# Blank rows written in 64 pieces on the sync engine's queue, and a routing phase re-ordered with one-pass products

## The chip, the core and the metric

One core of one Trainium2 chip runs the whole program. The metric is the device time of one execution in microseconds (us). The engines are TensorE (PE for products, PEld for its weight loads), VectorE (DVE), ScalarE (ACT), GpSimd (POOL) and the sync engine (SP), which here only issues DMAs. SP and POOL each have a DMA queue of their own; 16 DMA engines serve both.

## The reference

Two decoder layers over 64 sequences ("blocks") of 128 tokens and 256 features, all in float32:

```
x = x + mamba(layernorm(x))                  # layer 0: state-space mixer, 8 heads
x = x + cross_attention(layernorm(x), ctx)   #          16 heads with rotary positions
x = x + recurrence(layernorm(x))             #          gated recurrence over the 64 blocks
x = x + attention(layernorm(x))              # layer 1: grouped attention
x = x + cross_attention(layernorm(x), ctx)   #          one head of 256
x = x + experts(layernorm(x))                #          8 experts, 2 per token, one shared
```

The last line is the one that the routing phase serves:

```
scores = sigmoid(xf @ gate_w.T + lb_bias);  topw, topi = top_k(scores, 2)
topw = topw / (topw.sum(-1, keepdims=True) + 1e-8)
for e in range(8):
    m = topi == e
    wmean = (topw * m).sum() / max(m.sum(), 1)
    out = out + where(m.any(-1), mlp_e(xf) * wmean, 0)
out = out + mlp_shared(xf)
```

## The kernel before

The program is five phases, each with its own streams of instructions for the engines and a barrier of all engines at its end.

**start** loads and turns weights. **layer0** is a software pipeline over the 64 blocks (`pipeline` with `step(i)`: stage k of the pipeline works on block i - k), with a fixed hand-written order on every engine. **layer1** is a second such pipeline. **route** handles all 8192 tokens at once. **experts** first computes the shared expert for each block and scatters every token's row to the place in `pair_rows` (a DRAM buffer of 512 features and 4 further words per row) where tokens with the same pair of experts stand together; then it runs over 91 slots of 128 such rows and scatters the results to the output.

A slot may be filled only in part, so `pair_rows` must first hold blank rows: zeros, and a token number past the last one, so that the output's scatter drops them. In layer0 POOL does this: it fills the tiles `blank` and `blank_end` (L1460 to L1463), and issues 12 DMAs (L1469), 4 strided quarters of the buffer with three column ranges each, for 92 x 128 rows in all. Only behind these does POOL's stream come to its first step of the pipeline, `scale_tokens(0)` (L1477, L1480), which multiplies the mixer's inputs `m_xt_` of a block by their step sizes. TensorE's `m_mix` (L943) needs that product.

SP's step in layer0 has three parts: `load_sums(i)` (L881, 512 KB, a row of decay sums sent to all partitions of `m_E`; it waits for the mixer's products and squares of block i - 1), `store_output(i - 4)` (L890, which waits for ScalarE's last stage), and `load_context(i)` (L886, 128 KB). VectorE uses the sums at the start of its next step (`m_relative`, L1294), ahead of `m_residual` (L1330), the statistics, and the convolution (`m_convolve`, L1268, which waits for ScalarE's taps, L1108).

In route VectorE runs one chain in which nearly every instruction waits for the one before it (`link`). It waits for the constant table (L2127), builds the scores, the two best experts of each token and the number of its pair of experts (28 pairs), and from that `t_hot`, 64 x 28 ones and zeros per partition (L2143). TensorE counts each pair's tokens in each block (28 products of one column, L2078), VectorE spreads the counts with a triangular mask (L2147), and TensorE makes every token's rank among its pair (L2083, L2084: four groups of two float32 products of 448 columns each) and the pairs' totals (L2086). One semaphore, `t_rank`, releases VectorE behind all nine. VectorE then computes each pair's first slot (L2150 to L2156), the place of each token (L2159 to L2166), the slots' owners (L2167 to L2170), the shares and their sums per expert (L2172 to L2178), and, after a product that adds these over partitions (L2089), the mean weights (L2180 to L2187) and the owners' row (L2190).

Of the kernel before, what the change touches and what calls it, by code (L numbers as in the profile page):

```python
# [55 lines left out]
BLANKS = 4 * -(-SLOTS // 4)  # L56
# [4 lines left out]
def constant_table():  # L61
# [59 lines left out]
        t_table t_chain t_sig t_hot t_tiles t_prefix t_rank t_sums t_tot t_owner t_ownT  # L121
# [10 lines left out]
def decoder(nc, args, xo_dram, cum_dram, table, out):  # L132
# [8 lines left out]
    with ExitStack() as stack:  # L141
# [608 lines left out]
        slots = nc.dram_tensor("pair_rows", (BLANKS * P, ROW), F32, kind="Internal").ap()  # L750
# [122 lines left out]
        with phase("layer0") as block:  # L873
            @block.sync
            def _(e):
# [15 lines left out]

                def step(i):
# [566 lines left out]
            def _(e):  # L1459
# [56 lines left out]
                e.wait_ge(S["blank"], 12 * 16)  # L1516
# [526 lines left out]
        def by_pair(a):  # L2043
            return a.rearrange("p (b q) -> p b q", q=PAIRS)

        t_hot, t_prod = (by_pair(wk(NB * PAIRS)) for _ in range(2))
# [22 lines left out]
        with phase("route") as block:  # L2069
# [5 lines left out]
            def _(e):  # L2075
                e.wait_ge(S["t_hot"], 1)
                for q in range(PAIRS):
                    last = e.matmul(bank[7][0:NB, SPARE + q:SPARE + q + 1], t_hot[:, :, q], const[:, C_ONE:C_ONE + 1],  # L2078
                                    start=True, stop=True)
                last.then_inc(S["t_tiles"], 1)  # L2080
                e.wait_ge(S["t_prefix"], 1)
                for g in range(4):
                    e.matmul(bank[4 + g][:, 0:SPARE], r_up, t_hot[:, 16 * g:16 * g + 16, :], start=True, stop=False)  # L2083
                    e.matmul(bank[4 + g][:, 0:SPARE], const[0:NB, C_ONE:C_ONE + P], t_prod[0:NB, 16 * g:16 * g + 16, :],  # L2084
                             start=False, stop=True)
                e.matmul(bank[4][:, SPARE:SPARE + PAIRS], const[0:NB, C_ONE:C_ONE + P], t_tiles[0:NB], start=True, stop=True)\  # L2086
# [471 lines left out]
```

## Time and profile before

| | us |
|---|---|
| median of 3 runs | 3533.28 |
| lowest, highest | 3522.47, 3534.46 |
| the profiled execution | 3528.69 |
| its span | 3526.9 |

The span is the time that the profile's clock covers, 1.8 us less than the execution's own time. Of it TensorE is busy 88%, VectorE 79%, ScalarE 64%, POOL 43%. The phase layer0 begins near 91 us, route near 3022 us, and experts near 3087 us. A timeline row gives start, duration, engine, line, operation, and in brackets how long the engine had been idle before it and what released it; rows that follow each other on an engine with the same line are merged, with their number behind the x. PEclk is TensorE's granted clock as a share of 2.4 GHz.

### The profile page before, as it was taken

The page shows a single profiled execution, that of the slowest core. Times are in us where ns is not written, and L with a number is a line of the kernel's source. Part 1 is how long each engine was busy: PE and PEld are TensorE (multiplying, and loading weights), DVE is VectorE, ACT ScalarE, POOL GpSimd, SP SyncE. Part 2 cuts the span into 40 slices and gives each one's busy share as a digit, 9 for nine tenths or more (in the row PEclk, how much of TensorE's full clock was granted, in tenths as well). Part 3 has the DMA queues.
Part 4 walks back from the last instruction along what each step waited for, and adds up shares of the span by engine and source line. Part 5 has one row for each costly group of instructions (what it writes and reads, how often), then busy time and mean ns, then how long its engine had stood idle before and what let it go on. Part 6 is the DMA issues. An engine that isn't in the chain of part 4 may idle for free. (4 is left out here: it accounts for less than half of the span.)

```text
span 3526.9 us, 95395 instructions
## 1 busy us (share of the span) xinstructions
PE 3097.6 (88%) x27092; PEld 2670.7 (76%) x27093; DVE 2780.0 (79%) x8725; ACT 2267.1 (64%) x8246; POOL 1532.2 (43%) x5125
## 2 busy tenths in 40 slices
PE   6149999999999999999998689999999999399998
PEld 4047888888888888888887577777777777287998
DVE  5148888888888888888886478888888887488776
ACT  4026777777777777777776477777777777033333
POOL 1124445444444444544443145555555554033333
PEclk9569999999999999999999799999999999599999
DMA  6930000100100000000010100000000000022443
GB/s 181 218 84 28 32 27 28 34 27 27 36 27 27 33 30 27 30 33 27 27 36 14 59 18 16 18 18 15 18 18 18 15 18 14 2 88 109 136 139 91
DMA packets 92223, 162.13 MB, mean 46 GB/s; under 512 B 13379, under 2 KB 57776, under 8 KB 92144
## 3 DMA queue, kind: packets, MB, share of 16 engines
q1 hardware_dynamic: 73616, 102.32, 9.8%
q0 software_dynamic: 18528, 58.84, 5.7%
q8 instruction: 39, 0.64, 0.1%
q14 instruction: 40, 0.33, 0.0%
HBM read 102.85 MB, written 61.79 MB: 47 GB/s over the span
## 5 line engine op out<-in xcount | busy, mean ns | idle before, releaser
L386 POOL TENSOR_TENSOR tiny<-tiny 128x1 f32<-128x1 f32 x3456 | 779.6, 226 | 801.1 <-DVE tiny L373 560.4
L803 ACT ACTIVATE work<-bank,att 128x128 f32<-128x128 f32 x2048 | 722.2, 378 | 57.2 <-DVE att L793 51.2
L803 ACT ACTIVATION_READ_ACCUMULATOR work<-bank,att 128x1 f32 x2048 | 445.3, 217 | 0.0
L793 DVE TENSOR_REDUCE att<-bank 128x4 f32<-128x512 f32 x512 | 334.2, 684 | 45.6 <-PE bank L786 45.6
L822 PE MATMUL bank<-const,work 128*128 128x128 f32 x2048 | 317.1, 278 | 22.3 <-ACT work L803 18.2
L786 PEld LDWEIGHTS bank<-work 32*128 32x128 f32 x4096 | 253.7, 189 | 107.0 <-issue 74.6
L1268 DVE SCALAR_TENSOR_TENSOR work<-work,small 128x127 f32<-128x127 f32 (+2 forms) x1152 | 318.7, 345 | 9.9 <-ACT work L1108 5.2
L786 PE MATMUL bank<-work 32*128 32x128 f32 x4096 | 302.4, 286 | 20.1 <-ACT work L1153 2.5
L386 POOL TENSOR_TENSOR tiny<-tiny,const 128x1 f32<-128x1 f32 x1152 | 248.2, 215 | 90.2
L822 PEld LDWEIGHTS bank<-const,work 128*128 128x128 f32 x2048 | 238.6, 142 | 61.9 <-ACT work L803 38.7
L186 PE MATMUL bank<-w1r,workr 128*128 (+2 forms) x802 | 267.8, 334 | 0.4 <-issue 0.2
L186 PE MATMUL bank<-w0r,workr 128*128 128x256 f32 (+1 forms) x640 | 215.1, 336 | 43.9 <-DVE workr L1248 40.5
L206 PE MATMUL bank<-extra,w0p 128*128 128x128 f32 x1536 | 244.1, 282 | 2.8 <-ACT r_tfi_ L1169 1.8
L188 PE MATMUL bank<-w1r,workr 128*128 (+2 forms) x802 | 241.8, 302 | 0.0
L187 PE MATMUL bank<-w1r,workr 128*128 (+2 forms) x802 | 241.7, 301 | 0.0
L206 PE MATMUL bank<-d_state,w0p 128*128 128x128 f32 x1536 | 236.9, 277 | 0.0
L943 PE MATMUL bank<-work 128*128 128x64 f32 x1024 | 135.1, 278 | 90.0 <-POOL work L1477 88.7
L206 PEld LDWEIGHTS bank<-extra,w0p 128*128 128x128 f32 x1536 | 205.0, 194 | 11.3 <-ACT r_tfi_ L1169 2.1
L206 PEld LDWEIGHTS bank<-d_state,w0p 128*128 128x128 f32 x1536 | 205.0, 194 | 0.0
L943 PEld LDWEIGHTS bank<-work 128*128 128x128 f32 x1024 | 130.9, 201 | 90.9 <-issue 89.0
L188 PE MATMUL bank<-w0r,workr 128*128 128x256 f32 (+1 forms) x640 | 196.5, 307 | 0.0
L187 PE MATMUL bank<-w0r,workr 128*128 128x256 f32 (+1 forms) x640 | 196.2, 307 | 0.0
(357 smaller groups left out, 8486.2 us busy)
## 6 DMA issues: line engine op xcount, KB each, us to landing
work<-decay_sums SPq DMA_DIRECT2D x64, 512.0 KB, 3.6
pair_rows<-extra POOLq DMA_DIRECT2D x8, 2944.0 KB, 27.8
work<-pair_rows SPq DMA_DIRECT2D x91, 258.0 KB, 2.8
work<-in_ctx SPq DMA_DIRECT2D x128, 128.0 KB, 2.0
x_res<-in_x POOLq DMA_DIRECT2D x8, 1024.0 KB, 17.5
recurrence_out<-r_xo_ SPq DMA_DIRECT2D x64, 128.0 KB, 1.7
work<-recurrence_out SPq DMA_DIRECT2D x64, 128.0 KB
out_dram<-work POOLq DMA_INDIRECT x91
```

The lines of the kernel that those rows point to most:

```text
L186: pe.matmul(out_, lhs[0], rhs[0], start=first, stop=False)
L187: pe.matmul(out_, lhs[0], rhs[1], start=False, stop=False)
L188: return pe.matmul(out_, lhs[1], rhs[0], start=False, stop=last)
L206: last = pe.matmul(out_, w[:, k, n0:n0 + P], act[:, k, :], start=first and k == 0, stop=last_ and k == 1)
L386: e.tensor_tensor(out_, a_, b_, ALU.add if b_ is three_halves else ALU.mult)\
L786: mm = e.matmul(sc_banks[g % 2][:, c:c + P], qT[32 * g:32 * g + 32, odd, blk, :], kT[32 * g:32 * g + 32, blk, :], start=True, stop=True)
L793: e.tensor_reduce(a_nm[:, 4 * g:4 * g + 4], sc_banks[g % 2][:, :].rearrange("p (h k) -> p h k", k=P), AX.X, ALU.max, negate=True).then_inc ...
L803: last = e.activation(Pb[g % 2][:, c * P:c * P + P], sc_banks[g % 2][:, c * P:c * P + P], ACT.Exp, bias=a_nm[:, 4 * g + c:4 * g + c + 1], ...
L822: last = e.transpose(pt_banks[g % len(pt_banks)][:, h * P:h * P + P], Pb[g % 2][:, h * P:h * P + P], ident)
L943: last = e.matmul(bank[0][:, h * HD:h * HD + HD], m_E[:, h, :], m_xdt_[:, h * HD:h * HD + HD], start=True, stop=True)
L1268: last = e.scalar_tensor_tensor(out=m_acc[:, j, k:P], in0=m_raw_[:, j, 0:P - k], scalar=cw[:, j, CONV - 1 - k:CONV - k], in1=m_acc[:, j, k:P],
```

## The change

The buffer has 91 slots in place of 92, since each piece covers 91 x 128 / 64 = 182 rows. POOL still fills `blank` and `blank_end`, but its 12 DMAs, and its wait for them at the end of the phase, are gone. SP waits for the two tiles ahead of its pipeline, writes one piece of 182 rows in every step behind `load_context(i)`, with three DMAs, and waits for all 192 at the end.

```
-                e.wait_ge(S["blank_ready"], 2)
-                for k in range(4):
-                    rows_k = slots.rearrange("(s k p) d -> k p s d", k=4, p=P)[k]
-                    for at, n, of in ((0, D, blank), (D, D, blank), (2 * D, 4, blank_end)):
-                        e.dma_start(rows_k[:, :, at:at + n], of.unsqueeze(1).to_broadcast([P, BLANKS // 4, n]))\
-                            .then_inc(S["blank"], 16)
+                def blank_rows(b):
+
+                    n = SLOTS * P // NB
+                    rows_b = slots[0:NB * n].rearrange("(b p s) d -> b p s d", b=NB, p=n // 2)
+                    rows_b = rows_b[b] if isinstance(b, int) else rows_b[ds(b, 1)].rearrange("o p s d -> p (o s) d")
+                    for at, n_, of in ((0, D, blank), (D, D, blank), (2 * D, 4, blank_end)):
+                        e.dma_start(rows_b[:, :, at:at + n_], of[0:n // 2].unsqueeze(1).to_broadcast([n // 2, 2, n_]))\
+                            .then_inc(S["blank"], 16)
+
                     if live(b):
                         load_context(b)
-
+                    b = i
+                    if live(b):
+                        blank_rows(b)
+
+                e.wait_ge(S["blank_ready"], 2)
                 pipeline(e, 4, step)
                 e.wait_ge(S["r_store"], 16 * NB)
+                e.wait_ge(S["blank"], 3 * 16 * NB)
```

In route, `t_hot`, the counts and the masked counts are written as float32r in `w_s` and `workr` (the values are small whole numbers), with float32r copies of the ones and of the triangle that ScalarE makes. The ranks' groups go to banks 0 to 3, each with a count of `t_rank` of its own.

```
             def _(e):
+                e.wait_ge(S["t_ones"], 1)
                 e.wait_ge(S["t_hot"], 1)
                 for q in range(PAIRS):
-                    last = e.matmul(bank[7][0:NB, SPARE + q:SPARE + q + 1], t_hot[:, :, q], const[:, C_ONE:C_ONE + 1],
+                    last = e.matmul(bank[7][0:NB, SPARE + 2 * q:SPARE + 2 * q + 2], r_hot[:, :, q], r_one[:, 0:2],
                                     start=True, stop=True)
                 last.then_inc(S["t_tiles"], 1)
                 e.wait_ge(S["t_prefix"], 1)
+                e.matmul(bank[4][:, SPARE:SPARE + PAIRS], r_one[0:NB], r_tiles[0:NB], start=True, stop=True)\
+                    .then_inc(S["t_whole"], 1)
                 for g in range(4):
-                    e.matmul(bank[4 + g][:, 0:SPARE], r_up, t_hot[:, 16 * g:16 * g + 16, :], start=True, stop=False)
...
+                    e.matmul(bank[g][:, 0:SPARE], r_below, r_hot[:, 16 * g:16 * g + 16, :], start=True, stop=False)
+                    e.matmul(bank[g][:, 0:SPARE], r_one[0:NB], r_before[0:NB, 16 * g:16 * g + 16, :],
+                             start=False, stop=True).then_inc(S["t_rank"], 1)
...
             def _(e):
                 e.activation(t_s, logits, ACT.Exp, scale=-1.0).then_inc(S["t_sig"], 1)
+                e.activation(r_one, const[:, C_ONE:C_ONE + P], ACT.Copy)
+                e.wait_ge(S["t_table"], 16)
+                e.activation(r_below, r_up, ACT.Copy).then_inc(S["t_ones"], 1)
```

VectorE's wait for the table stands just ahead of `t_hot`; the shares stand behind it, the owners, the shares' sums and the two comparisons with the experts' numbers behind the pairs' first slots, and the last products and sums of the mean weights have no `link` between the two halves.

What stands in a row on SP in the loop of layer0 before:

```order
L881 ISA
L881 DMA work<-decay_sums 128x1024
L889 REGISTER_ALU
L890 ISA
L890 DMA recurrence_out<-r_xo_ 128x256
L886 ISA
L886 DMA work<-in_ctx 128x256
L179 REGISTER_ALU
```

and now:

```order
L880 ISA
L880 DMA work<-decay_sums 128x1024
L888 REGISTER_ALU
L889 ISA
L889 DMA recurrence_out<-r_xo_ 128x256
L885 ISA
L885 DMA work<-in_ctx 128x256
L897 ISA
L897 DMA pair_rows<-extra 182x1x256
L897 ISA
L897 DMA pair_rows<-extra 182x1x256
L897 ISA
L897 DMA pair_rows<-work 182x1x4
L178 REGISTER_ALU
```

Three DMAs stand between a block's context and the next block's decay sums, which the loop comes to next.

On POOL, at the start of layer0, before (the last rows are `scale_tokens(0)`):

```order
L1463 IOTA work 128x1
L1469 DMA pair_rows<-extra 128x23x256
L1469 DMA pair_rows<-extra 128x23x256
L1469 DMA pair_rows<-work 128x23x4
L1469 DMA pair_rows<-extra 128x23x256 x2
L1469 DMA pair_rows<-work 128x23x4
L1469 DMA pair_rows<-extra 128x23x256 x2
L1469 DMA pair_rows<-work 128x23x4
L1469 DMA pair_rows<-extra 128x23x256 x2
L1469 DMA pair_rows<-work 128x23x4
L1477 TENSOR_TENSOR work<-work,tiny 128x512
```

and now:

```order
L1476 IOTA work 128x1
L1484 TENSOR_TENSOR work<-work,tiny 128x512
L1487 TENSOR_TENSOR work<-work,small 128x512
```

Nothing of POOL's own stands ahead of the first block's work any more.

On VectorE, in route, from the counts to the places of the tokens, now:

```order
L2169 TENSOR_TENSOR workr<-work,w_s 64x1792
L2174 TENSOR_SCALAR work<-bank 128x28
L2175 TENSOR_SCALAR work<-work 128x28
L2176 TENSOR_SCALAR work<-work 128x28
L2178 TENSOR_TENSOR work<-work 128x28 x5
L2180 TENSOR_TENSOR work<-work 128x28
L2181 TENSOR_TENSOR work<-work 128x28
L2183 TENSOR_TENSOR work<-work 128x27 x2
L2184 TENSOR_REDUCE work<-work 128x2
L2186 TENSOR_REDUCE work<-work 128x8
L2187 TENSOR_REDUCE work<-rows 128x8
L2189 TENSOR_TENSOR work<-const,work 128x512 x2
```

L2181 to L2189 stood behind the places before; now they stand ahead of the first instruction that needs the ranks.

## Rows read from the trace of the kernel before

**Rows 1.** Stretches: length; busy PE, PEld, DVE, ACT, POOL (instructions); PEclk; DMA share; GB/s.
```profile
108.00:199.00 91.00, 1.54 (x6) 1.25 (x6) 3.23 (x5) 2.02 (x4) 10.78 (x8) 0.50 0.89 195
...
3022.00:3086.00 64.00, 22.20 (x78) 11.75 (x78) 36.15 (x68) 0.63 (x1) 0.00 (x0) 0.50 0.01 2
```

**Rows 2.** Waits by engine, line and releaser, 92 to 320 us: total, times, longest.
```profile
PE bank L943 <- POOL work L1477: 88.7, 1, 88.7
...
DVE work L1294 <- DMA work<-decay_sums: 11.8, 2, 9.0
```

**Rows 3.** Timeline of POOL, start of layer0.
```profile
146.99 1.48 POOL L1469 DMA_DIRECT2D pair_rows<-work  x1 [47.35 <-issue]
...
195.59 1.48 POOL L1469 DMA_DIRECT2D pair_rows<-extra  x1 [41.21 <-issue]
...
198.57 1.05 POOL L1477 TENSOR_TENSOR work<-work,tiny 128x512 f32<-128x512 f32 x1
```

**Rows 4.** Timeline of all engines, blocks 0 and 1 of layer0.
```profile
110.61 0.60 ACT L1125 ACTIVATE work<-bank 128x512 f32<-128x512 f32 x1 [2.20 <-PE bank L932]
...
205.67 0.33 SPq L881 DMA_DIRECT2D work<-decay_sums  x1
...
214.69 2.41 ACT L1108 ACTIVATE work<-work,small 128x128 f32<-128x128 f32 x6
216.41 0.87 DVE L1294 TENSOR_SCALAR work<-work,tiny 128x128 f32<-128x128 f32 x4 [9.04 <-DMA work<-decay_sums]
...
219.62 5.02 DVE L1268 SCALAR_TENSOR_TENSOR work<-work,small 128x127 f32<-128x127 f32 x18
```

**Rows 5.** Timeline of one steady step of layer0.
```profile
1016.63 0.33 SPq L886 DMA_DIRECT2D work<-in_ctx  x1
...
1018.94 0.33 SPq L881 DMA_DIRECT2D work<-decay_sums  x1
...
1023.70 0.88 DVE L1294 TENSOR_SCALAR work<-work,tiny 128x128 f32<-128x128 f32 x4
...
1025.67 0.48 DVE L1330 SCALAR_TENSOR_TENSOR x_res<-bank,tiny,x_res 128x256 f32 x1 [0.76 <-POOL tiny L386]
...
1045.64 0.33 SPq L881 DMA_DIRECT2D work<-decay_sums  x1
```

**Rows 6.** Line L881, the decay sums' load (64 issues).
```profile
DMA to landing us min/median/max: 3.3/3.6/10.7
```

**Rows 7.** Timeline of route: ScalarE and VectorE up to the counts.
```profile
3022.19 0.63 ACT L2098 ACTIVATE work<-tab 128x512 f32<-128x512 f32 x1 [2.76 <-PEq L157]
...
3026.43 0.42 DVE L2131 TENSOR_SCALAR work<-work 128x512 f32<-128x512 f32 x1
...
3042.41 6.55 PEld L2078 LDWEIGHTS bank<-const,work 128*64 128x64 f32 x56 [22.01 <-DVE work L2143]
```

**Rows 8.** Timeline of VectorE in route, from the counts on.
```profile
3049.08 0.18 DVE L2146 TENSOR_SCALAR work<-bank 64x28 f32<-64x28 f32 x1 [6.73 <-PE bank L2078]
...
3066.06 0.19 DVE L2150 TENSOR_SCALAR work<-bank 128x28 int32<-128x28 f32 x1 [14.74 <-PE bank L2086]
...
3068.06 2.21 DVE L2159 SCALAR_TENSOR_TENSOR work<-work,bank 128x448 f32<-128x448 f32 x4
...
3074.53 0.18 DVE L2167 TENSOR_TENSOR work<-work 128x28 f32<-128x28 f32 x1
...
3075.32 0.22 DVE L2172 TENSOR_TENSOR work<-work 128x64 f32<-128x64 f32 x1
...
3077.84 1.07 DVE L2177 TENSOR_REDUCE work<-work 128x8 f32<-128x512 f32 x1
...
3080.70 0.17 DVE L2180 TENSOR_SCALAR work<-bank 128x8 f32<-128x8 f32 x1 [0.70 <-PE bank L2089]
```

**Rows 9.** Timeline of TensorE, float32r products of 512 columns right after route.
```profile
3090.77 0.63 PE L188 MATMUL bank<-w1r,workr 128*128 128x512 f32 x1
3091.20 0.63 PE L186 MATMUL bank<-w1r,workr 128*128 128x512 f32 x1
```

More of the change, by code:

```diff
@@ L748, in decoder @@
         r_T = wk(D).rearrange("p (k t) -> p k t", k=2)
-        slots = nc.dram_tensor("pair_rows", (BLANKS * P, ROW), F32, kind="Internal").ap()
+        slots = nc.dram_tensor("pair_rows", (SLOTS * P, ROW), F32, kind="Internal").ap()
         blank, blank_end = wk(D), wk(4)
@@ L1515, in _ @@
                 pipeline(e, 5, step)
-                e.wait_ge(S["blank"], 12 * 16)
         layer0_weights.close()
@@ L2044, in by_pair @@
             return a.rearrange("p (b q) -> p b q", q=PAIRS)
-        t_hot, t_prod = (by_pair(wk(NB * PAIRS)) for _ in range(2))
+        t_prod = by_pair(wk(NB * PAIRS))
+        r_hot = by_pair(w_s[:, 0:NB * PAIRS])
+        t_hot = r_hot.bitcast(F32)
+        at_ = NB * PAIRS
+        r_one, r_below, r_tiles = w_s[:, at_:at_ + P], w_s[:, at_ + P:at_ + 2 * P], w_s[:, at_ + 2 * P:at_ + 2 * P + PAIRS]
+        r_before = by_pair(wr(NB * PAIRS))
         t_s, t_first, t_second = (by_tile(wk(NT)) for _ in range(3))
@@ L2126, in _ @@
                     e.memset(ends, 0.0)
-                e.wait_ge(S["t_table"], 16)
-                e.tensor_scalar(where[:, :, 2].bitcast(I32), r_tok, 1.0, None, ALU.mult)
                 e.wait_ge(S["t_sig"], 1)
@@ L2166, in _ @@
                 e.tensor_scalar(where[:, :, 3].bitcast(I32), t_place, 1.0, None, ALU.mult)
-                link(e.tensor_tensor(t_gone, r_slot.to_broadcast([P, PAIRS]), t_ends[5][:, HALF:], ALU.is_ge))
-                for c in range(2):
-                    link(e.tensor_tensor(t_step[:, c, 0:PAIRS - 1], t_gone[:, 0:PAIRS - 1], r_step[c], ALU.mult))
-                e.tensor_reduce(t_owner, t_step[:, :, 0:PAIRS - 1], AX.X, ALU.add).then_inc(S["t_owner"], 1)
-                link(e.tensor_tensor(t_rcp, t_max, t_max2, ALU.add))
-                link(e.tensor_scalar(t_rcp, t_rcp, 1e-8, None, ALU.add))
-                link(e.reciprocal(t_rcp, t_rcp))
-                link(e.tensor_tensor(t_s, t_s, t_mask, ALU.mult))
-                link(e.tensor_tensor(t_s, t_s, wide(t_rcp), ALU.mult))
-                link(e.tensor_reduce(t_sums[:, 0:E], t_s.rearrange("p b e -> p e b"), AX.X, ALU.add))
-                e.tensor_reduce(t_sums[:, E:2 * E], t_mask.rearrange("p b e -> p e b"), AX.X, ALU.add).then_inc(S["t_sums"], 1)
                 e.wait_ge(S["t_tot"], 1)
@@ L2183, in _ @@
                                             in1=t_mean[:, E:2 * E], op0=ALU.mult, op1=ALU.mult))
-                for c, key in enumerate((t_upper, t_lower)):
-                    link(e.tensor_tensor(t_tmp, across(const[:, C_IOTA:C_IOTA + E]), wide(key), ALU.is_equal))
-                    link(e.tensor_tensor(t_tmp, t_tmp, across(t_mean[:, 0:E]), ALU.mult))
-                    link(e.tensor_reduce(where[:, :, c], t_tmp, AX.X, ALU.add))
+                for c, is_ in enumerate((t_first, t_second)):
+                    e.tensor_tensor(is_, is_, across(t_mean[:, 0:E]), ALU.mult).then_inc(S["t_chain"], 1)
+                for c, is_ in enumerate((t_first, t_second)):
+                    n += 1
+                    e.wait_ge(S["t_chain"], n)
+                    e.tensor_reduce(where[:, :, c], is_, AX.X, ALU.add)
                 e.wait_ge(S["t_ownT"], 1)
```

43 lines of the change are left out of this document (28 added, 15 removed).

## The prediction

> **What bounds the kernel now.** I read the profile in three steps. First the busy time by stretch. TensorE is busy 88% of the span, so most of the program is a full pipeline; what matters are stretches in which every engine is idle. Two stand out [rows 1]: from 108 to 199 us nothing computes (TensorE 1.5 us busy of 91, VectorE 3.2) while the DMA engines are 89% busy, and from 3022 to 3086 us, the routing phase, VectorE is busy 36 of 64 us and TensorE 22, at a granted clock of 0.50, the lower of its two levels (1.2 GHz). The change touches just these two, and adds work to a third stretch, the steady steps of layer0, which are 1045.64 - 1018.94 = 26.7 us each [rows 5].
>
> Second, who ends the first hole. The list of waits says that TensorE's mixer product L943 waited 88.7 us, once, for POOL's L1477 [rows 2]. POOL's own timeline shows why: its blank-row DMAs take 1.48 us each to issue, but twice its stream stands still in the middle of them, 47.35 and 41.21 us, with no other engine named [rows 3]: I read this as waiting for room in its queue. Only at 198.57 us does it come to L1477, although L1477's input, ScalarE's L1125, was there at 110.61 + 0.60 = 111.21 us [rows 4].
>
> Third, the waits inside route: VectorE stands 6.73 us for the counts and 14.74 us for ranks and totals [rows 8].
>
> **The change, part 1: the first block.** POOL has only two memsets and an iota ahead of L1477, so this starts when its input is there, at about 111.3 us instead of 198.57: **-87.3 us**. What follows at once (L943) waited for L1477 alone, so all of it moves. What is late next is block 1's decay sums. They were issued at 205.67 and VectorE waited 9.04 us for them, to 216.41 [rows 4], since they took 10.7 us to land against a median of 3.6 [rows 6]: the last blank DMAs were still running. With 3.6 us they land 7.1 us sooner, but the convolution (219.62) also needs ScalarE's taps, which end at 214.69 + 2.41 = 217.10 whatever the sums do. So the step gains at most 219.62 - 217.10 = **-2.5 us**. The new wait of SP for the blank tiles comes before its first load and delays it by under 1 us; what depends on that load ends in L1268 of block 0, which waits for the taps anyway. I cost it at nothing, at most +0.7.
>
> **Part 2: 61 steady steps.** The blanks have not gone; SP writes them, three DMAs per step. The nearest issue costs are 0.33 us each [rows 5], and setting each address adds up to 0.1 as the rows of SP's own loop stand (ISA ahead of DMA), so 1.3 us in all, behind the context's DMA, whose issue ends at 1016.96. The next decay sums were issued at 1018.94, a gap of 1.98. The issue cost therefore fits with 0.7 us to spare; SP's next instruction, and all queued behind it, is as early as now.
>
> The data also share the DMA engines with these sums. A piece is 182 rows x 2064 bytes = 376 KB. The same rows went out before at 195 GB/s with 89% of the engines' time, that is 219 GB/s at full use [rows 1], so a piece takes 1.7 us. The sums are 524 KB: 2.4 us at that rate, of their 3.6 us, so about 1.2 us passes before data flow. The piece then flows from 1018.2 to 1019.9, and the sums from 1020.1: they hardly meet. If the whole piece stood ahead, the sums would land 1.7 us late. What covers this: they land at 1018.94 + 3.6 = 1022.5, VectorE comes to them at 1023.70 (L1294) with no wait, 1.2 us later, and then idles 0.76 us for POOL at L1330 [rows 5]. So **1.9 us** of lateness costs VectorE nothing that it doesn't wait for now. If the cover goes, each microsecond more costs up to 61 us over the phase. I take +2.5 us in total for the odd collision; bounds 0 and, at 0.5 us per step beyond the cover, +30.
>
> The DMA's rows are 91 partitions read twice and 182 rows written. The Trainium skill (DMA: Bandwidth & Descriptors, section "Why a DMA increments its semaphore by 16 and not by 1") says that a DMA of the sync queue runs on the largest number up to 16 of DMA engines that divides the outermost size of both sides, which here is 13. By it the piece takes 16/13 as long, 2.1 us instead of 1.7 as an estimate from the same row, and the time of the forecast stays. No row of this trace shows it, since the DMAs of layer0 have 128 rows.
>
> **Part 3: route.** Durations by VectorE's timeline, step by step.
> - Table: L2131 starts at 3026.43, behind the table's DMA and a copy; the scores' input, ScalarE's L2098, ends at 3022.82 [rows 7]. It can start near 3022.9: **-3.5 us**. The table is now needed some 15 us later and has long landed. ScalarE's two copies end well before too.
> - Counts: 56 weight loads in 6.55 us, two for each float32 product, 0.117 each [rows 7]. A float32r product has one load and one pass, so 28 x 0.117 = 3.3, plus 0.2 for the semaphores: 3.5 instead of 6.73, **-3.2 us**. Below this the shares set the end: L2172 to L2176, 3075.32 to 3077.84 = 2.5 us [rows 8], plus a copy, now run in this wait, so they leave the chain: **-2.5 us**.
> - Ranks: VectorE waited 14.74 us for L2086, the ninth product. Now the pairs' totals come first, one product of 28 columns: I take 0.6 us. **-14.1 us**. Behind it TensorE has eight products of 448 columns. Float32r products of 512 columns follow each other in 0.43 us at this clock [rows 9], so 448 columns take 0.38 and eight 3.0, 5 us at most if each weight load adds to it. VectorE has until then: first slots 3066.06 to 3068.06 (2.0), owners 3074.53 to 3075.32 (0.8), sums 3077.84 to 3080.0 (2.1) [rows 8], and two comparisons of about 0.65: 6.2 us. So the ranks are there first, and owners and sums cost what they did.
> - The end: the wait of 0.70 us for the sums' product [rows 8] is covered by the tokens' places, **-0.7**, and four links less save **-0.4**.
>
> Route together: 3.5 + 3.2 + 2.5 + 14.1 + 0.7 + 0.4 = **24.4 us** of 64.
>
> **Sum.** 3528.7 (the profiled execution) - 87.3 - 2.5 - 24.4 + 2.5 = **3417 us**. The median of the runs before is 4.6 us above that execution and their lowest 6.2 below, so the same holds for the outcome within about 5 us.
>
> **Rivals.**
> - *Cover partly gone.* The sums land later than 1.9 us in each step: 0.5 us beyond it costs 61 x 0.5 = 30, 3447 us. For it: the pieces go out directly ahead of them, and a step had none there before. Against it: the gap of 1.98 us on SP, and 1.2 us before VectorE looks [rows 5]. 12%.
> - *Slower than before.* The same place, but the piece holds the queue for long: the 1 KB writes of SP's queue run at a quarter of the rate seen on POOL's, 6.8 us a piece, from 1018.2 to 1025.0. The sums start 4.9 us late, less the cover of 1.9 is 3.0, times 61 is 183: 3528.7 - 114.2 + 183 = 3598 us. It turns the sign where the sums land 3.8 us late (1.9 beyond the cover, 61 x 1.9 = 116), a piece of 5.7 us. Against it: the rate at which the same rows left before [rows 1], 1.7 us a piece. 3%.
> - *The hole is only moved.* Something else holds block 0, an input that the wait for POOL hid, so that 55 of the 87 us come back: 3450. Against it: L943's wait names POOL alone, and L1477's own input was 87 us early [rows 2, 4]. 3%.
> - *Route falls short.* The float32r products of few columns run no faster than the float32 ones did. Counts and half of the ranks' time return, 10 us: 3427. 5%.
> - Forecast as it stands: 77%.
>
> **How the numbers follow.** The range must reach from the full gain with no collision and the clock held up by a shorter idle time (3400) to the first rival with some more (3458). It leaves the slower rival out, and the rare case between. A measurement of this kernel tells about 0.5% from no change, 18 us. Faster by more than that: all cases but the slower one and a little of the first beyond its price, 0.96; within it 0.01; slower 0.03.
>
> **What would show it.** L1477 of block 0 near 112 us, and no stretch of idle engines after it; block 1's L1294 waits about 2 us or less. In a steady step SP's load of the sums still issues about 2 us behind the context's, lands within 5.5 us, and VectorE does not wait for it; the step stays as long as it is. Route takes 40 us, with a wait of some 3.5 us at the counts, under 1 us at the totals and none at the ranks. I am wrong if VectorE's L1294 waits for the decay sums in every step, or if POOL is late for another reason.

## The result: 3413.5 us for 3533.0, and where the time went

| | before | after |
|---|---|---|
| median | 3533.02 | 3413.51 |
| lowest, highest | 3522.47, 3534.46 | 3412.63, 3418.98 |
| the profiled execution | 3528.69 | 3413.31 |
| its span | 3526.9 | 3411.5 |

The ratio of the mean times is 0.967, with an interval of 0.965 to 0.969 (the ratios below are of means too, and the times are medians). The forecast was 3417 in a range of 3400 to 3458. Between the two profiled executions the span fell by 115.4 us. The starts of the phases (first DMA of layer0, first instructions of layer1, route and experts) divide it:

| part | before | after | difference | forecast |
|---|---|---|---|---|
| start phase | 91.26 | 93.04 | +1.8 | 0 to +0.7 |
| layer0, first step (blocks 0 and 1) | 137.35 | 47.70 | -89.65 | -89.8 |
| layer0, steps 2 to 4 | 93.44 | 87.48 | -6.0 | 0 |
| layer0, 59 steps | 26.698 each | 26.779 each | +5.1 | +2.5 |
| layer0, last steps | | | -1.5 | 0 |
| layer1 | 1046.6 | 1046.1 | -0.6 | 0 |
| route | 64.61 | 39.52 | -25.1 | -24.4 |
| experts | 440.0 | 440.6 | +0.5 | 0 |

The steps are measured between the issues of two context loads on SP. The length given for a steady step, here and below, is the mean of the last 58 of the 59; the difference in the table is that of all 59. Three readings of the profile after carry this table.

**The hole is gone.** Timeline of all engines of the changed kernel, blocks 0 and 1 of layer0 (start, duration, engine, line, what it does, and in brackets how long the engine was idle before it and for whom):

```profile
112.18 1.04 POOL L1484 TENSOR_TENSOR work<-work,tiny 128x512 f32<-128x512 f32 x1 [19.17 <-ACT work L1138]
...
119.80 0.34 SPq L880 DMA_DIRECT2D work<-decay_sums  x1
...
123.17 0.87 DVE L1307 TENSOR_SCALAR work<-work,tiny 128x128 f32<-128x128 f32 x4 [1.69 <-DMA work<-decay_sums]
...
131.75 0.35 DVE L1281 SCALAR_TENSOR_TENSOR work<-work,small 128x127 f32<-128x127 f32 x1 [4.73 <-ACT work L1121]
```

POOL's first work of block 0, which stood at 198.57 [rows 3], now waits for ScalarE and starts with its input, at 112.18. Block 1's decay sums are waited for 1.69 us, where it was 9.04 [rows 4], and the convolution behind them waits for ScalarE's taps (L1121), as the forecast said. The windows show it by engine. Stretches of the changed kernel: length; busy PE, PEld, DVE, ACT, POOL (instructions); PEclk; DMA share; GB/s:

```profile
108.00:130.00 22.00, 15.22 (x68) 13.10 (x68) 11.45 (x31) 5.61 (x12) 6.82 (x25) 0.57 0.07 25
...
141.00:169.00 28.00, 21.11 (x126) 17.51 (x126) 19.97 (x56) 14.25 (x47) 9.34 (x28) 0.76 0.13 37
169.00:197.00 28.00, 21.55 (x183) 17.44 (x183) 21.61 (x63) 18.69 (x63) 10.04 (x29) 0.94 0.13 38
197.00:228.60 31.60, 28.66 (x255) 24.89 (x254) 27.27 (x84) 24.37 (x83) 17.08 (x51) 1.00 0.10 34
...
2927.00:2967.00 40.00, 11.65 (x47) 7.64 (x47) 32.95 (x65) 1.52 (x4) 0.00 (x0) 0.50 0.02 4
```

In 22 us from 108 on TensorE is busy 15.2, where it was 1.5 in 91 [rows 1]. The middle three rows are steps 2 to 4; the same three of the kernel before:

```profile
228.00:256.00 28.00, 20.74 (x128) 16.33 (x127) 20.22 (x57) 14.25 (x48) 9.48 (x28) 0.80 0.07 25
256.00:287.00 31.00, 24.61 (x182) 19.93 (x181) 21.38 (x63) 18.59 (x63) 10.31 (x29) 0.83 0.06 22
287.00:322.00 35.00, 32.18 (x260) 28.31 (x258) 27.65 (x85) 25.09 (x84) 17.09 (x52) 0.90 0.06 20
```

The work is the same, but the granted clock reaches 0.94 and 1.00 in the second and third of them where it was 0.83 and 0.90. That is where the -6.0 us lie; two other executions of the same layer0, `changed_again` and `pieces_alone`, don't have them (below).

**The steady steps have a new wait, which hardly costs anything.** Timeline of SP and VectorE of the changed kernel, one steady step:

```profile
1005.07 0.34 SPq L885 DMA_DIRECT2D work<-in_ctx  x1
1005.59 2.01 SPq L897 DMA_DIRECT2D pair_rows<-extra  x2
1007.81 0.89 SPq L897 DMA_DIRECT2D pair_rows<-work  x1
1009.29 0.35 SPq L880 DMA_DIRECT2D work<-decay_sums  x1
...
1012.74 0.87 DVE L1307 TENSOR_SCALAR work<-work,tiny 128x128 f32<-128x128 f32 x4 [0.73 <-DMA work<-decay_sums]
```

and waits of VectorE (232 to 1860 us) and of TensorE (229 to 1809 us) in the same kernel, as total, times, longest:

```profile
DVE work L1307 <- DMA work<-decay_sums: 56.3, 59, 1.3
...
DVE x_res L1343 <- POOL tiny L385: 1.7, 2, 1.4
```

```profile
PE bank L821 <- ACT work L802: 7.6, 28, 0.5
```

Before, VectorE's waits of the same stretch (320 to 1960 us) had no decay sums among them, but

```profile
DVE x_res L1330 <- POOL tiny L386: 46.3, 60, 1.4
```

The sums were issued 1018.94 - 1016.63 = 2.31 us behind the context [rows 5] and are now issued 4.22 behind it, 1.91 later. They land in the usual time from their issue (line L880, issue to landing):

```profile
DMA to landing us min/median/max: 3.3/3.6/4.2
```

So VectorE waits some 0.95 us for them in each step, and in exchange no longer waits 0.77 us for POOL a moment later. What is left reaches TensorE in some of the steps as a short wait for ScalarE (L802), and these steps are the longer ones: the 28 steps with such a wait take 26.90 us on average, the 31 without it 26.68.

**Route.** VectorE's first instruction in route, before:

```profile
3022.25 0.36 DVE L2126 MEMSET work<- 128x44 f32 x6 [1.55 <-PEq L157]
```

Timeline of VectorE and TensorE of the changed kernel, from the first instruction to the places of the tokens:

```profile
2931.40 0.36 DVE L2141 MEMSET work<- 128x44 f32 x6 [1.54 <-PEq L156]
2932.00 0.43 DVE L2143 TENSOR_SCALAR work<-work 128x512 f32<-128x512 f32 x1 [0.24 <-ACT work L2110]
...
2948.05 3.32 PEld L2090 LDWEIGHTS bank<-w_s 128*64 128x64 f32 x28 [18.49 <-issue]
...
2951.56 0.18 DVE L2167 TENSOR_SCALAR w_s<-bank 64x28 fp32r<-64x28 f32 x1 [1.12 <-PE bank L2090]
...
2954.28 0.19 DVE L2174 TENSOR_SCALAR work<-bank 128x28 int32<-128x28 f32 x1 [0.48 <-PE bank L2094]
...
2954.84 0.28 PEld L2098 LDWEIGHTS bank<-workr,w_s 64*128 64x128 f32 x1 [0.38 <-issue]
2954.84 0.74 PE L2098 MATMUL bank<-workr,w_s 64*128 64x448 f32 x1
...
2958.86 0.74 PE L2098 MATMUL bank<-workr,w_s 64*128 64x448 f32 x1
...
2960.25 2.20 DVE L2193 SCALAR_TENSOR_TENSOR work<-work,bank 128x448 f32<-128x448 f32 x4
```

The wait for the counts fell from 6.73 to 1.12 us, that for ranks and totals from 14.74 to 0.48 [rows 8], and the instruction that needs the ranks (2960.25) waits for nothing. In the window 2927 to 2967 above, VectorE is busy 33 of 40 us; it was 36 of 64 [rows 1].

### The profile page after: what moved, and what is told of

Same layout as the page of the kernel before. It is cut to its first block and busy times, and to the rows that moved or that the text cites. A ratio compares the mean times of both kernels' runs of the same rounds, so it can differ in the third digit from the quotient of the medians.

```text
span 3411.5 us, 95859 instructions
## 1 busy us (share of the span) xinstructions
PE 3081.2 (90%) x27055; PEld 2659.9 (78%) x27056; DVE 2776.1 (81%) x8725; ACT 2258.2 (66%) x8248; POOL 1512.2 (44%) x5113
## 5 line engine op out<-in xcount | busy, mean ns | idle before, releaser
L385 POOL TENSOR_TENSOR tiny<-tiny 128x1 f32<-128x1 f32 x3456 | 773.3, 224 | 800.0 <-DVE tiny L372 559.2
L802 ACT ACTIVATE work<-bank,att 128x128 f32<-128x128 f32 x2048 | 720.1, 377 | 55.9 <-DVE att L792 50.1
L802 ACT ACTIVATION_READ_ACCUMULATOR work<-bank,att 128x1 f32 x2048 | 444.5, 217 | 0.0
L821 PE MATMUL bank<-const,work 128*128 128x128 f32 x2048 | 317.9, 278 | 30.6 <-ACT work L802 25.8
L385 POOL TENSOR_TENSOR tiny<-tiny,const 128x1 f32<-128x1 f32 x1152 | 251.6, 218 | 90.2
L205 PE MATMUL bank<-extra,w0p 128*128 128x128 f32 x1536 | 242.9, 281 | 3.0 <-ACT r_tfi_ L1182 1.7
L205 PE MATMUL bank<-d_state,w0p 128*128 128x128 f32 x1536 | 235.7, 276 | 0.0
L205 PEld LDWEIGHTS bank<-extra,w0p 128*128 128x128 f32 x1536 | 203.7, 193 | 11.4 <-ACT r_tfi_ L1182 2.1
L205 PEld LDWEIGHTS bank<-d_state,w0p 128*128 128x128 f32 x1536 | 203.9, 193 | 0.0
L1501 POOL TENSOR_TENSOR x_res<-x_res,rows 128x256 f32 (+1 forms) x64 | 46.7, 729 | 343.4 <-DVE work L1264 343.4
L205 PE MATMUL bank<-work,w0p 128*128 128x128 f32 x1536 | 185.6, 278 | 0.5 <-ACT work L1107 0.5
```

The costliest lines, as they stand in the source:

```text
L205: last = pe.matmul(out_, w[:, k, n0:n0 + P], act[:, k, :], start=first and k == 0, stop=last_ and k == 1)
L385: e.tensor_tensor(out_, a_, b_, ALU.add if b_ is three_halves else ALU.mult)\
L802: last = e.activation(Pb[g % 2][:, c * P:c * P + P], sc_banks[g % 2][:, c * P:c * P + P], ACT.Exp, bias=a_nm[:, 4 * g + c:4 * g + c + 1], ...
L821: last = e.transpose(pt_banks[g % len(pt_banks)][:, h * P:h * P + P], Pb[g % 2][:, h * P:h * P + P], ident)
L1501: e.tensor_tensor(x_res[:, ds(b * D, D)], x_res[:, ds(b * D, D)], bo2_row, ALU.add).then_inc(S["c_x1b"], 1)
```

## The experiments

The kernels ran in three groups, each on one chip with the kernel before beside it. Group 1, `pieces_alone`, `route_alone`, `pieces_behind_sums` and `pieces_192`: before 3525.2 us (3518.0 to 3531.2). Group 2, `changed_again`, `pieces_behind_sums_again`, `one_dma_piece` and `one_dma_behind_sums`: 3538.4 (3526.8 to 3542.3). Group 3, the other four: 3526.3 (3523.3 to 3531.2).

**One half at a time.** `pieces_alone` is the kernel before with the blank rows in pieces, and the old route:

```diff
+                    b = i
+                    if live(b):
+                        blank_rows(b)
...
-                for k in range(4):
-                    rows_k = slots.rearrange("(s k p) d -> k p s d", k=4, p=P)[k]
```

> The kernel before with the blank-row part of the change alone; route as before. Theory (the parts add, layer0 gave 92 us and route 25): 3413.5 + 25 = 3438 us. Rival (part of the 25 us in route came from layer0's pieces, for instance by another granted clock or buffer): clearly off 3438 by more than 5 us. In its profile route should again last 64.6 us from the first memset to the first instruction of experts, and the steps of layer0 should jitter between 26.6 and 27.1 us as they do in the changed kernel.

Measured: 3440.8 us (3439.6 to 3443.3), ratio 0.976 [0.974, 0.978].

`route_alone` is the changed kernel with POOL's 12 DMAs back:

```diff
-                    b = i
-                    if live(b):
-                        blank_rows(b)
...
+                for k in range(4):
+                    rows_k = slots.rearrange("(s k p) d -> k p s d", k=4, p=P)[k]
```

> The changed kernel with POOL's 12 large blank DMAs put back; route as changed. Theory: 3533 - 25 = 3508 us; the hole of 88 us is back in front of L1477's successor, the steady steps are 26.70 us each without jitter, and route lasts 39.5 us. Rival (the two parts share a gain): under 3500 or over 3516.

Measured: 3506.4 us (3503.5 to 3508.0), ratio 0.994 [0.993, 0.996]. The hole was back (first step 137.03 us), and the steady steps were 26.730 us with no wait for sums. In `pieces_alone` the steps were 26.779 us as in the changed kernel, with 53.7 us of waits for sums in 59 steps. The two gains are 84.4 and 18.8 us, together 103 of about 116 (3.3% of that chip's 3525). Both times lie near the expected 3438 and 3508, but these were worked out from 3533 and 3413; against this chip's 3525 each gain is smaller than expected, 84 for 95 and 19 for 25. Of the missing 13 us 8.8 are seen in one place of the profiled executions: steps 2 to 4 of `pieces_alone` took 31.2, 30.6 and 34.5 us, 96.3 together against 87.5 in the profile after. The rest isn't settled. Route took 39.52 us in `route_alone`, as in the changed kernel, but 63.08 in `pieces_alone`, where 64.6 was expected: VectorE waited 2.19 us for the constant table there and 3.71 before, with the same instructions. So 1.5 of the 25.1 us depend on when the table lands in an execution of the old route. The two halves act in separate phases, and both are needed for the whole.

**What delays the sums: SP's issue time, or the data?** Four kernels tell them apart. `pieces_behind_sums` issues the same three DMAs behind the sums' load in the step:

```diff
                         load_sums(b)
+                        blank_rows(b)
...
-                    b = i
-                    if live(b):
-                        blank_rows(b)
```

> The changed kernel with the three DMAs of a piece moved on SP from behind the context's load to behind the decay sums' load, ahead of the wait of some 20 us for ScalarE's last stage. Theory (the pieces' issue time of 3 x 0.9 us on SP makes the next sums late, which uses up VectorE's cover and makes the steps jitter): VectorE's waits for the sums in the steady steps go from 56 us to about 0, its 46 us of waits for POOL at the residual come back, the steps are 26.70 us again, and the time falls by 58 x 0.085 = 5 us, to 3408. Rival (the jitter comes from the DMA traffic or from memory, wherever it is issued): the waits for the sums go but the steps stay at 26.79 us and the time at 3413.

Measured: 3414.1 us (3411.3 to 3414.5), ratio 0.968 [0.966, 0.970]; steps 26.729 us. The steps are nearly those of the theory (26.70); the time is not its 3408, and the changed kernel did not run on this chip to compare it with. Timeline of its SP:

```profile
1013.04 0.34 SPq L885 DMA_DIRECT2D work<-in_ctx  x1
1015.33 0.34 SPq L880 DMA_DIRECT2D work<-decay_sums  x1
1015.85 2.02 SPq L897 DMA_DIRECT2D pair_rows<-extra  x2
```

The three issues take as long as ever, but the sums are on time (2.29 us behind the context), VectorE's waits for them are 0.4 us in all and its wait for POOL is back, 46.6 us in 60 times. TensorE's new waits for L802 are gone.

`pieces_192` keeps the place and makes a piece of 192 rows (96 partitions twice) in place of 182 (91 twice):

```diff
+BLANKS = 96
...
-        slots = nc.dram_tensor("pair_rows", (SLOTS * P, ROW), F32, kind="Internal").ap()
+        slots = nc.dram_tensor("pair_rows", (BLANKS * P, ROW), F32, kind="Internal").ap()
...
-                    n = SLOTS * P // NB
+                    n = BLANKS * P // NB
```

> The changed kernel with a buffer of 96 slots, so that a piece is 96 partitions x 2 = 192 rows instead of 91 x 2 = 182; DMAs and their place as they are. Theory A (a count of rows that 16 doesn't divide is what makes an issue on SP cost 0.90 us against 0.33 of a load of 128 rows): issues near 0.35 us, VectorE's waits for the sums fall from 1 us per step to under 0.2, and the time falls by about 5 us to 3408. Theory B (the source's third dimension or the number of rows makes it): issues stay near 0.9 us or rise with 192/182 to 0.95, time 3413 to 3416.

Measured: 3413.2 us (3405.8 to 3417.1), ratio 0.967 [0.965, 0.970]; steps 26.732 us. Timeline of its SP:

```profile
1012.89 0.34 SPq L886 DMA_DIRECT2D work<-in_ctx  x1
1013.41 1.40 SPq L898 DMA_DIRECT2D pair_rows<-extra  x2
...
1016.16 0.34 SPq L881 DMA_DIRECT2D work<-decay_sums  x1
```

With 5% more rows, a DMA takes 0.6 to 0.7 us to issue in place of 0.9 to 1.05. That lies between the two theories, 0.35 and 0.9, and the time is again not the 3408 of theory A. The sums are 3.27 us behind the context, 0.96 later than before, and this is inside the 1.2 us by which they used to be early: VectorE waits 5.3 us for them, 15 times. The change of size that adds data takes the wait away, so it is the issue time that makes it.

`one_dma_piece` keeps the place and 182 rows, but writes a whole row from one tile, in one DMA:

```diff
-        blank, blank_end = wk(D), wk(4)
+        blank = layer0_weights.enter_context(nc.sbuf_tensor("blank_row", [P, ROW], F32))[:, :]
+        blank_end = blank[:, 2 * D:ROW]
...
-                    for at, n_, of in ((0, D, blank), (D, D, blank), (2 * D, 4, blank_end)):
-                        e.dma_start(rows_b[:, :, at:at + n_], of[0:n // 2].unsqueeze(1).to_broadcast([n // 2, 2, n_]))\
-                            .then_inc(S["blank"], 16)
+                    e.dma_start(rows_b, blank[0:n // 2].unsqueeze(1).to_broadcast([n // 2, 2, ROW])).then_inc(S["blank"], 16)
```

> The changed kernel with a tile of one whole blank row (516 words), so that a piece is one DMA of 182 rows of 2064 bytes instead of three; its place, behind the context's load, is as changed. Theory (what made the sums late is SP's time to issue three DMAs, 2.7 us, more than the gap of 2.0): one issue of 0.9 us fits the gap, VectorE's waits for the sums fall from 56 us to under 10, steps are 26.73 us flat, and the time is 3 to 5 us under changed_again. Rival (the piece's data ahead of the sums make them late): waits of 0.5 us or more per step remain, since the bytes are the same.

Measured: 3410.7 us (3406.8 to 3417.1), ratio 0.964 [0.963, 0.966]; steps 26.710 us. Its SP, and VectorE's waits (232 to 1860 us):

```profile
1001.82 0.34 SPq L886 DMA_DIRECT2D work<-in_ctx  x1
1002.35 0.92 SPq L897 DMA_DIRECT2D pair_rows<-blank_row  x1
1004.13 0.35 SPq L881 DMA_DIRECT2D work<-decay_sums  x1
```

```profile
DVE work L1306 <- DMA work<-decay_sums: 22.6, 57, 2.1
```

VectorE's waits fell to 22.6 us, not to the expected 10 or less: both the theory and its rival hold in part. One issue costs what each of three did, so the sums are issued on time, 2.31 us behind the context. But now they take longer to land. Line L881 of this kernel, 400 to 1800 us:

```profile
DMA to landing us min/median/max: 4.7/5.0/6.6
```

That is 1.3 to 1.4 us over the 3.6 and 3.7 of the others: this is what the piece's data do when they stand directly ahead of the sums. Both mechanisms exist; in the changed kernel the slow issues spread the data out so far that only the first acts.

`one_dma_behind_sums` joins both edits:

```diff
                         load_sums(b)
+                        blank_rows(b)
...
+                    e.dma_start(rows_b, blank[0:n // 2].unsqueeze(1).to_broadcast([n // 2, 2, ROW])).then_inc(S["blank"], 16)
```

> Both edits: one DMA per piece, and that behind the decay sums' load. Theory: nothing is left to gain beyond either alone, steps 26.73 us, 3 to 5 us under changed_again. It is the version that I would expect to be the fastest by a little.

Measured: 3412.8 us (3405.3 to 3413.9), ratio 0.964 [0.963, 0.965]; steps 26.697 us, one wait for sums of 0.4 us. It is not the fastest by anything that the times can tell.

To compare these closely, the changed kernel (`changed_again`) and `pieces_behind_sums` ran again on that same chip, unaltered.

> The changed kernel again, beside the three below on one chip. In the profile that I have of it, the three steps after the first block took 28.4, 27.3 and 31.8 us (granted clock 0.76, 0.94, 1.00), in four other kernels' profiles 31.2, 30.6 and 34.6 with the same instructions. Theory (the clock rises at another time from run to run, worth up to 9 us, and this is most of the scatter): its steady steps average 26.78 us in any case, and the time lies between 3408 and 3420. Rival (the short steps belong to this kernel): they are again under 29 us.

Measured: 3421.2 us (3413.3 to 3425.2), ratio 0.966 [0.965, 0.968]; steps 26.843 us, 59.8 us of waits for sums; steps 2 to 4 took 31.1, 30.5 and 31.8 us, 93.4 together, at granted clocks of 0.66, 0.80 and 1.00. The median is 1 us above the expected 3408 to 3420, and the steps are longer than 26.78.

> The three DMAs of a piece behind the decay sums' load, again, beside the changed kernel on the same chip. Its steady steps were 26.73 us flat, those of the changed kernel jitter around 26.79. Theory (the late sums cost VectorE 3.5 to 5 us over the phase): 3 to 5 us under changed_again. Rival (nothing that a time can show): within 2 us of it.

Measured: 3411.8 us (3405.8 to 3414.1), ratio 0.963 [0.962, 0.965]; steps 26.716 us.

Beside each other, the changed kernel is 8.3 to 10.5 us above the three versions of this group that let the sums go on time or nearly so. The 59 steps account for 7.3 to 8.4 us in the profiled executions, where 3 to 5 had been expected. The two kernels with one DMA also had short steps 2 to 4 in their profiles (87.7 and 87.5 us), so the clean pair is `changed_again` and `pieces_behind_sums_again`, both with 93.4 or 93.5: their profiled executions are 8.3 us apart, 7.3 of it in the 59 steps. The whole difference is 0.3%, and only the interval of `pieces_behind_sums_again` lies clear of the changed kernel's, by 0.0001; the steps' lengths and waits, which agree in all runs, bear it better than the medians.

**Another place for the same DMAs.** `pieces_on_pool` gives the pieces to POOL, behind its last mixer work of the step:

```diff
                         scale_tokens(b)
+                        blank_rows(b)
```

> The changed kernel with the same 64 pieces issued by POOL on its own queue, behind each block's scale_tokens, instead of by SP. It asks whether the pieces or the other queue removed the hole. Theory (POOL stood still because its queue had no room for more than five of the large DMAs; pieces of 182 rows leave room): L1477's successor starts near 112 us, no wait of POOL at an issue of more than 2 us, and 3413 to 3425, since three issues of 0.6 to 1.5 us per step now stand in front of POOL's roots, for which VectorE waits 0.76 us a step already; if 1.5 us each, up to 58 x 2 = 116 us slower than that. Rival (POOL's issuing as such holds it up, whatever the size): hole or long waits in every step, over 3500.

Measured: 3483.9 us (3476.5 to 3484.2), ratio 0.988 [0.986, 0.990]. No hole (first step 47.38 us), but steps of 27.866 us, so the time is well above the 3413 to 3425 of the theory and inside what it allowed for slow issues. Timeline of its POOL, and VectorE's longest waits over the whole span:

```profile
1011.63 1.41 POOL L1471 DMA_DIRECT2D pair_rows<-extra  x2
1012.83 0.92 POOL L1471 DMA_DIRECT2D pair_rows<-work  x1
1013.42 0.86 POOL L385 TENSOR_TENSOR tiny<-tiny 128x1 f32<-128x1 f32 x2
```

```profile
DVE work L1250 <- POOL tiny L385: 96.4, 63, 4.7
```

The 2.3 us of issues stand ahead of the inverse roots (L385) that VectorE waits for, and 1.1 to 1.2 us of them come through in each step. The same DMAs cost 2.7 us on SP (three of 0.9), of which 0.09 to 0.14 comes through. What matters is who is queued behind them, not how long they take.

`bulk_on_sp` leaves them in 12 large DMAs, issued by SP behind its work of the first step:

```diff
+                def blank_all():
+                    e.wait_ge(S["blank_ready"], 2)
+                    for k in range(4):
...
+                pipeline(e, 4, step, 0, blank_all)
```

> The changed kernel with the 12 large blank DMAs (92 x 128 rows) back, but issued by SP behind step 0 of its pipeline. It asks whether the hole came from POOL being held, or from the traffic of 24 MB in front of the next loads. Theory (both: with POOL free, L1477's successor starts near 112 us, but block 1's decay sums stand behind 24 MB in SP's queue until about 200 us): the hole moves to VectorE's wait for the sums, the time is within 15 us of 3413 + 80 = 3493. Rival (POOL's standing still was all): block 1 goes on as in the changed kernel, under 3430.

Measured: 3498.6 us (3497.3 to 3500.1), ratio 0.992 [0.990, 0.994]. POOL is free at once (its first mixer work at 111.21), and the hole comes back in another place:

```profile
92.91 7.22 SPq L909 DMA_DIRECT2D pair_rows<-extra  x2
...
187.19 12.26 SPq L909 DMA_DIRECT2D pair_rows<-work  x1
...
199.93 10.50 SPq L881 DMA_DIRECT2D work<-decay_sums  x1
...
214.01 0.87 DVE L1304 TENSOR_SCALAR work<-work,tiny 128x128 f32<-128x128 f32 x4 [93.50 <-DMA work<-decay_sums]
```

SP is held at its issues until 199.9 and the sums of block 1 go out only then. So moving the DMAs off POOL is not what removes the hole; cutting them into pieces that follow the work is.

**Route's two parts.** `float32_new_order` keeps the changed kernel's order and puts float32 products back:

```diff
-        r_hot = by_pair(w_s[:, 0:NB * PAIRS])
...
+        r_hot, r_before, r_one = t_hot, t_prod, const[:, C_ONE:C_ONE + P]
```

> The changed kernel with the counts, totals and ranks as float32 products again (table of ones and triangle used as they are), everything else, VectorE's order above all, as changed. Theory: counts take 6.7 us again, of which 2.6 are covered: +3.2; eight rank products of 1.79 us behind the totals last 14.3 us, of which VectorE's 6.0 us of other work and the first three groups' places cover all but 6.5: +6.5, and 0.4 for the totals. Route 39.5 + 10 = 49.5 us. So order alone saves 15 of the 25 us. Rival (the order hides nothing because the products are what takes the time): 55 us or more.

Measured: 3427.8 us (3425.6 to 3430.9), ratio 0.972 [0.970, 0.974]; route 49.69 us. Two of its waits on VectorE:

```profile
2960.59 0.18 DVE L2161 TENSOR_SCALAR work<-bank 64x28 f32<-64x28 f32 x1 [4.29 <-PE bank L2087]
...
2974.28 0.62 DVE L2187 SCALAR_TENSOR_TENSOR work<-work,bank 128x448 f32<-128x448 f32 x1 [2.96 <-PE bank L2095]
```

`one_pass_old_order` has the one-pass products of the changed kernel and the order of before on VectorE and TensorE. The totals, for one, go behind the ranks again:

```diff
-                e.matmul(bank[4][:, SPARE:SPARE + PAIRS], r_one[0:NB], r_tiles[0:NB], start=True, stop=True)\
-                    .then_inc(S["t_whole"], 1)
...
+                e.matmul(bank[4][:, SPARE:SPARE + PAIRS], r_one[0:NB], r_tiles[0:NB], start=True, stop=True)\
+                    .then_inc(S["t_rank"], 1)
```

> The changed kernel with float32r products, but VectorE's order in route and the place of the totals behind the ranks as before. Theory: table +3.5 less what ScalarE's end hides (it ends at 2.1 us after VectorE could start here: +2.2), shares +2.5 less the 1.1 that VectorE now waits for the counts: +1.4, ranks 8 x 0.67 + 0.4 instead of 0.5 us: +5.3, sums' product +0.7, links +0.4: route 39.5 + 10 = 49.5 us. So one-pass products alone save 15 of the 25 us, and the two parts overlap by 5. Rival (parts add): 39.5 + 10 would need the other run at 54.6 us.

Measured: 3428.4 us (3422.0 to 3431.0), ratio 0.972 [0.971, 0.974]; route 50.21 us. Its two waits:

```profile
2952.51 0.18 DVE L2161 TENSOR_SCALAR w_s<-bank 64x28 fp32r<-64x28 f32 x1 [3.56 <-PE bank L2090]
...
2960.28 0.19 DVE L2166 TENSOR_SCALAR work<-bank 128x28 int32<-128x28 f32 x1 [5.54 <-PE bank L2098]
```

Alone the order saves 14.9 us of the 64.6 and the products save 14.4, both together 25.1. They overlap by 4.2 us, since both work on the same wait: the new order hides products behind VectorE's own work, and the one-pass products leave less to hide.

## Why the prediction was right, and where it was not

**Block 0 and block 1** (-89.8 forecast, -89.65 measured). Right in total. The first part gave a little more (88.2 us from the start of layer0, for 87.3), the second less: from POOL's first work to the convolution it is 131.75 - 112.18 = 19.57 us, and was 219.62 - 198.57 = 21.05 [rows 3, 4], so 1.5 us where 2.5 were counted. The taps that set its end came 1.0 us later behind POOL's work than before. Half of it is a wait that the hole had hidden: TensorE's L956 (before L943) needs VectorE's L1316 besides POOL's product, and starts 1.65 us behind POOL's first work (113.83 - 112.18) where it was 1.16 (199.73 - 198.57), so "waited for L1477 alone" was not quite right. The other half is TensorE's 24 products ahead of the taps (L205), which take 4.09 us for 3.60, at a granted clock of 0.61 over the products just ahead and these for 0.66. The rival "the hole is only moved" fell with the profile after: block 0 ran through. `bulk_on_sp` shows what such a moved hole looks like.

**The start phase** (+1.8, at most +0.7 forecast). SP's wait for the blank tiles took 0.6 us of it. The other 1.2 us lie ahead of layer0, where the change does nothing: SP's last DMA of the start phase is issued at 87.81 before and 89.00 after, and the same DMA lies anywhere from 86.75 to 90.27 in the traces of the other kernels. So it is scatter.

**The steady steps.** This is the step of the prediction that failed in its working, though the sum hardly shows it. "1.3 us in all" for three issues came from the 0.33 us of loads with 128 rows. Line L897 of the changed kernel, min/median/max in ns:

```profile
L897 SPq DMA_DIRECT2D pair_rows<-extra x128: 858/899/1047, 93.9 to 1810.5; - x128
L897 SPq DMA_DIRECT2D pair_rows<-work x64: 851/886/886, 95.9 to 1811.6; - x64
```

The third of them ends 3.3 us behind the end of the context's issue (1008.70 and 1005.41), and the sums' issue follows 0.6 later, where the whole gap was 1.98. So "SP's next instruction is as early as now" was wrong, and so was "VectorE does not wait for it": the prediction's own sign of being wrong, a wait of L1294 (now L1307) for the sums in every step, is there in 59 of 59. What saved the number was the other half of the same paragraph: 1.9 us of lateness costs VectorE nothing. The lateness was 1.91 us by the issues and up to 0.1 by the landing. Of this 1.2 us was earliness that went unused before, and 0.77 the wait for POOL, so the cover is used up. What goes beyond it shows in TensorE's waits for ScalarE (L802): 28 steps with such a wait, 26.90 us on average, and 31 without, 26.68, where all were near 26.70, make the +5.1. In the second run 38 steps have it, 10.7 us in all, and the steps cost 7.3 over the version with the sums on time. That an issue time wrong by a factor of nearly three ended just at the edge of the cover, and not beyond it, was luck. The rival "cover partly gone" had the right mechanism and was kept small by that edge: by its own price each further 0.5 us would have cost 30.

The other half of the term, the data, was sized fairly: a piece directly ahead of the sums was put at 1.7 us of lateness, and `one_dma_piece` shows 1.3 to 1.4. But that kernel has just the timing that the prediction assumed, the piece's issue inside the gap and the sums issued on time, for which it said that piece and sums "hardly meet". They do meet; the late issue kept them apart in the changed kernel, and the cover held in both (steps of 26.710 in `one_dma_piece`).

On the shape: each DMA of a piece of 182 rows (91 partitions twice) issues in 0.90 us, and one of 192 rows (96 twice) in 0.60. The Trainium skill (DMA: Bandwidth & Descriptors, section "Why a DMA increments its semaphore by 16 and not by 1") has the first on 13 DMA engines and the second on 16, since 91 isn't divisible by 16 and 96 is; no trace here shows the engines of one DMA. The prediction worked out from it a piece of 2.1 us; no run shows how long a piece's data run, only that they hold the sums up by 1.3 to 1.4. The section says nothing of issue time; the runs fit a cost that depends on that number, but two shapes alone don't show that it does. That 192 rows still cost more than the 0.34 us of a load from 128 partitions stays open too.

**Steps 2 to 4** (-6.0, not forecast). The range allowed for "the clock held up by a shorter idle time", and the granted clock did rise earlier in this execution. But in `changed_again` the same three steps took 93.4 us, as before the change, and in `pieces_alone` 96.3. Over all traces without the hole they take 87.5 to 87.7 us three times, 93.4 or 93.5 three times and 96.1 to 96.4 five times, and in the three with a hole 93.4, 94.3 and 95.8. So the 6 us can't be counted on; whether the short form can occur behind a hole is not shown.

**Route** (-24.4 forecast, -25.1 measured), by item:
- Table: from VectorE's first instruction to the scores 3026.43 - 3022.25 = 4.18 us before [rows 7] and 0.60 now, -3.6 for -3.5. As said above, 1.5 of this is the table's late landing in that execution.
- Counts and shares: the loads took 3.32 us for 3.3, and the wait fell by 6.73 - 1.12 = 5.6 for 3.2 + 2.5 = 5.7. The sign to look for, "a wait of some 3.5 us", contradicted that sum: the shares lie inside the 3.5, so that 1.0 had to be left.
- Totals: 0.48 us for 0.6.
- Ranks: no wait, as forecast, but by less than thought. The eight products follow each other in 0.67 us, not in 0.38, and last 5.4 us (2954.17 to 2959.60), over the "5 us at most". In [rows 9] too each product has a weight load of its own, but there it runs beside the product before it:

```profile
3090.77 0.33 PEld L186 LDWEIGHTS bank<-w1r,workr 128*128 128x128 f32 x1
```

  The product of this load starts at 3091.20. In route load and product start together (both 2954.84 above), and 0.28 or 0.29 us of load and 0.38 of product make the 0.67; why the load isn't earlier there stays open. The last group's ranks end at 2959.60 and VectorE's fourth instruction needs them near 2961.9, so with 2.3 us less work on VectorE a wait would show; `float32_new_order`, whose products are slower, has three waits there, 0.59, 2.96 and 2.96.
- The end: no wait for the sums' product, -0.7 as forecast, and some -0.9 is left for the fewer links, where 0.4 was counted.

So the number was good because the large terms rested on rows that named the cause. That it came within 4 us is luck in part: -7.5 us in steps 2 to 4 and the last steps and +4.4 in the start and the steady steps, neither foreseen, cancel for the most part.

## What to carry to other kernels

A queue that issues DMAs is an engine with a program order: before many DMAs go on one, look at what stands behind them there, and cut them to what the steps can hide. Take the issue time from a DMA of the same shape, not from the nearest line. Work whose wait nobody can shorten (here counts and ranks) is best shortened and covered at once, and the two gains overlap; sum them from one timeline, not apart.

## What the runs showed of the hardware

- SP's issue time depends on the shape, not on the bytes: 0.90 us for 182 rows of 1024 or of 16 bytes, 0.92 for 182 of 2064, 0.6 to 0.7 for 192, 0.34 for 128. POOL issues the 182 rows in 0.71 and 0.92 us.
- An issue can hold the engine that makes it far longer when transfers pile up: POOL 47.35 and 41.21 us [rows 3]; in `bulk_on_sp` SP up to 19.08 us for a pair of issues, and 10.50 us for a load of sums that takes 0.33 otherwise.
- One-pass products of 448 columns came every 0.67 us in route at the granted clock of 0.50 (the 1.2 GHz level), each behind its own weight load of 0.28 or 0.29; the 512 columns of [rows 9] came every 0.43 us, with loads of 0.33 that ran beside the product before.
- The first full steps vary with their granted clock: three steps took 87.5 us (0.76, 0.94, 1.00), 93.4 (0.66, 0.80, 1.00) and 96.3 (0.66, 0.80, 0.90) in three executions of the same work.
